# A selective-scan and mixture-of-experts kernel on one core: the part ahead of the first scan in another order, and the LayerNorm passes of batch 0 dealt out over more slots

## What is computed

```
h = in_proj_w @ ctx            # per batch: 1024 channels x 1024 time steps, contraction 512
u = silu(conv1d_4taps(h) + conv_b)
dt_lo, B, C = split(x_proj_w @ u)           # 32, 16 and 16 rows
delta = softplus(dt_proj_w @ dt_lo + dt_proj_b);  A = -exp(A_log)
state[t] = exp(delta*A)*state[t-1] + delta*u*B[t]      # 16 states for each channel
y = (sum_n C[n]*state[n] + D*u) * silu(z),   z = layernorm(x)        # "LN1"
x = x + y^T
x = x + expert_ffn(layernorm(x))            # "LN2": logits, top 2 of 8, GELU, w3
```

## Time and profile before

| | |
|---|---|
| three runs | 2397.72, 2400.32, 2401.14 us (median 2400.32) |
| profiled execution | 2398.25 us, its span 2395.8 us |
| busy: PE, DVE, ACT, POOL | 2085.5, 2036.6, 1609.8, 1542.7 us |
| mean granted TensorE clock | 0.939 |
| chain that ended last | PE 46%, DVE 18%, issue 16%, ACT 15%, POOL 4% |

### The profile page before, as it was taken

The page is one execution under the profiler, slowest core; times in us unless marked ns, Lnnn a source line. Parts: engine busy times, 40 slices in busy tenths (PEclk is TensorE's granted clock), DMA queues, the critical chain, the costliest instruction groups (busy, mean ns, idle before and its releaser), DMA issues.

```text
span 2395.8 us, 34926 instructions
## 1 busy us (share of the span) xinstructions
PE 2085.5 (87%) x11828; PEld 1308.9 (55%) x11828; DVE 2036.6 (85%) x2540; ACT 1609.8 (67%) x2381; POOL 1542.7 (64%) x1089
## 2 busy tenths in 40 slices
PE   7798889988978987998978997798887897797999
PEld 2677677766654553445665554344665454344444
DVE  5899799989997899999998899998999789899311
ACT  2687877767769869656759967855677757854500
POOL 0598777778765765667766675676776577577111
PEclk9899989998989988998989998999898998899999
DMA  5311625664612844566722653566552265478512
GB/s 179 125 45 53 222 79 159 194 211 165 233 53 102 304 149 129 176 208 220 260 66 90 238 186 124 168 220 208 198 198 67 69 227 167 151 226 290 203 62 70
DMA packets 201891, 388.93 MB, mean 162 GB/s; under 512 B 30801, under 2 KB 96337, under 8 KB 201714
## 3 DMA queue, kind: packets, MB, share of 16 engines
q1 hardware_dynamic: 198544, 386.23, 48.0%
q10 hardware_dynamic: 3170, 0.47, 0.1%
HBM read 352.56 MB, written 34.08 MB: 161 GB/s over the span
## 4 chain that ended last, share of the span: by engine, by line
PE 46%; DVE 18%; issue 16%; ACT 15%; POOL 4%; DVEq 0%; DMA 0%; ACTq 0%; POOLq 0%; SPq 0%
PE dense L1243 12%; PE dense L1060 9%; DVE h L1624 8%; PE dense L1046 5%; PE dense L1000 5%; ACT dA L1350 4%; DVE dense L1600 3%; PE dense L1226 3%; POOL h L942 3%; ACT L1319 2%; PE dense L1021 2%; DVE u L1463 2%; PE dense L1012 2%; PE dense L1163 2%; PE dense L1067 2%
## 5 line engine op out<-in xcount | busy, mean ns | idle before, releaser
L942 POOL TENSOR_TENSOR h<-h,Cb 128x1024 f32<-128x1024 f32 x512 | 1209.2, 2362 | 359.3 <-DVE h L1624 333.3
L1350 ACT ACTIVATE dA<-delta,Av 128x512 f32<-128x512 f32 x1024 | 700.1, 716 | 336.0 <-DVE h L1624 333.2
L1624 DVE TENSOR_TENSOR_SCAN h<-dA,state,dense 128x512 f32<-128x512 f32 x512 | 627.9, 1265 | 20.5 <-PE dense L1060 9.6
L1624 DVE TENSOR_TENSOR_SCAN h<-dA,dense 128x512 f32<-128x512 f32 x512 | 596.9, 1205 | 40.0 <-PE dense L1060 22.8
L1060 PE MATMUL dense<-ident,h 128*128 128x128 f32 x4096 | 570.2, 289 | 42.4 <-POOL h L942 42.2
L1060 PEld LDWEIGHTS dense<-ident,h 128*128 128x128 f32 x4096 | 496.4, 150 | 177.5 <-issue 89.5
L1600 DVE TENSOR_TENSOR dense<-dense,Bb 128x512 f32<-128x512 f32 x720 | 458.7, 683 | 0.8
L1046 PE MATMUL dense<-Bb,duT 128*128 128x128 f32 x2432 | 354.6, 296 | 108.9 <-DVE h L1624 104.1
L1046 PEld LDWEIGHTS dense<-Bb,duT 128*128 128x128 f32 x2432 | 317.4, 205 | 161.2 <-issue 159.6
L1243 PE MATMUL dense<-w3h,xT 128*128 128x512 f32 x832 | 384.8, 598 | 0.8 <-DVE xT L1581 0.8
L1243 PEld LDWEIGHTS dense<-w3h,xT 128*128 128x128 f32 x832 | 148.9, 193 | 138.7 <-issue 137.4
(11 more groups left out here) (169 smaller groups left out, 2046.1 us busy)
## 6 DMA issues: line engine op xcount, KB each, us to landing
sww<-in_sw SPq DMA_DIRECT2D x167, 512.0 KB, 4.2
Cb<-bc_scratch SPq DMA_DIRECT2D x64, 512.0 KB, 6.9
Bb<-bc_scratch SPq DMA_DIRECT2D x59, 512.0 KB, 5.0
w3h<-in_sw SPq DMA_DIRECT2D x52, 512.0 KB, 8.4
w3h<-in_w3T SPq DMA_DIRECT2D x52, 512.0 KB, 5.0
row<-x_scratch SPq DMA_DIRECT2D x40, 512.0 KB, 4.7
xz<-in_x SPq DMA_DIRECT2D x64, 256.0 KB, 4.6
xt<-in_x SPq DMA_DIRECT2D x64, 256.0 KB, 4.2
```

What stands on the lines that cost most here:

```text
L942: e.tensor_tensor(h[:, s:s + 2, :], h[:, s:s + 2, :], Cb[:, 2 * q:2 * q + 2, :], ALU.mult).then_inc(prod_done, 1)
L1350: e.activation(dA[:, i % RA, :], delta[:, st % 2, :], ACT.Exp, scale=Av[:, j * N + n:j * N + n + 1]).then_inc(dA_done, 1)
L1624: e.tensor_tensor_scan(h[:, 2 * ((PAIRS * g + q) % RH) + n % 2, :], dA[:, (N * g + n) % RA, :], dense[:, BANKS.bank[("product", g, n)], :] ...
```

## The change

It has three groups of edits.

1. **Order ahead of the first scan.** TensorE begins with 13 matmuls on the constant tile `ones`, into bank M1, which nothing reads. Then all eight in_proj blocks, then all eight x_proj pieces, the first softplus matmul, the transposes of B, and only then in_proj of J and J+1 (bank F2 instead of F1), the turn of du, now in bank S. The transposes of B go to bank YT, so they wait for the convolution of block 4, and the first sum in YT waits for VectorE's diagonals. ScalarE does the first tap of the next block ahead of a silu; table load and exp(A_log) come before the row split; the first taps of J and J+1 move into slots 0 and 1 of step 0. VectorE keeps three LN1 rows between the convolutions, does rows 3 to 6 behind the last, and row 7 behind the softplus; the convolutions of J and J+1 move between the scans of slots 1 and 2.
2. **Diagonals.** VectorE makes only four (`DVE_DIAGONALS`), those of pairs 1 and 2. For pairs 4, 5 and 6 B is loaded and GpSimd makes them, as in later halves, in slots 0 to 3 behind the product with C. There are 14 loads in place of 11.
3. **LN1 of batch 1, made during batch 0.** The passes stand in slots 57, 58, 66, 69, 71, 74, 77 and 79, power in 83 and shift in 85. The first row load of batch 0's logits moves from slot 80 to 82. Batches 1 and 2 keep their slots.

```diff
+DVE_DIAGONALS = 2 * 2
+FIRST_LN1_ROWS = ((54, 57), (55, 58), (60, 66), (63, 69), (67, 71), (70, 74), (72, 77), (75, 79))
+WARM = 13
...
-        uses = [FIRST_S + 1, 2, 2, 1, 1, 1, 1, 1]
+        uses = [FIRST_S + 1, 2, 1, 2, 1, 1, 1, 1]
...
-                rows.append((b, 54 + 3 * k // 2, "ln1", k))
-                self.add(b, 57 + 3 * k // 2, "ln1_stats", k)
-            self.add(b, 69, "ln1_rstd")
-            self.add(b, 71, "ln1_shift")
+                load, t = (54 + 3 * k // 2, 57 + 3 * k // 2) if b else FIRST_LN1_ROWS[k]
+                rows.append((b, load, "ln1", k))
+                self.add(b, t, "ln1_stats", k)
+            self.add(b, 69 if b else 83, "ln1_rstd")
+            self.add(b, 71 if b else 85, "ln1_shift")
...
+        def by_dve(c, n):
+
+            return c == 0 and on_pe(0, n) and diag_index(0, n) < DVE_DIAGONALS
...
# GpSimd
+                if c == 0:
+                    e.wait_ge(diag_done, 1 + DVE_DIAGONALS)
...
             edges(0)
+            du_of(0, 1 + FIRST_S + 1)
             ln1_rstd(0)
-            du_of(0, 1 + FIRST_S + 1)
...
-                        if j == 0 and at == SLOTS + q and c and on_pe(g, n):
+                        if j == 0 and at == SLOTS + q and on_pe(g, n) and not by_dve(c, n):
                             diagonal_b(c, n)
...
# TensorE
+            e.wait_ge(masks, 1 + MASKS)
+            for i in range(WARM):
+                e.matmul(dense[:, M1, 0:P], ones[:], ones[:], start=True, stop=True)
             e.wait_ge(ctx_loaded, 1 + 16)
             for G in range(J):
                 e.wait_ge(first_win_loaded[G], 1 + 16)
                 first_in_proj(G, G, first_win[G], ctxs)
-                if G >= 2:
-                    first_x_proj(G - 2)
-            first_x_proj(J - 2)
...
+            for k in range(J):
+                first_x_proj(k)
             e.wait_ge(ident_step, 3)
             before_softplus(0, 0, FIRST_S)
...
             turn_b(0, FIRST_S)
+            e.wait_ge(first_ctx_loaded, 1 + 16)
+            for G, bank in ((J, F0), (J + 1, F2)):
+                e.wait_ge(win_loaded[G % 2], 1 + 16)
+                e.wait_ge(evac[bank], 1 + 1)
+                first_in_proj(G, bank, win[:, G % 2], first_ctx)
+            e.wait_ge(evac[S], 1 + FIRST_S + 1)
+            turn_du(0, S)
             times_b_at(2)
...
# ScalarE
-            for G in range(J):
-                tap_one(G, G, 0, 0, G)
-                silu_u(G, G, 1)
-            tap_one(J, F0, 0, 1, 0)
-            split_rows(0)
+            for G in range(J + 1):
+                if G < J:
+                    tap_one(G, G, 0, 0, G)
+                if G:
+                    silu_u(G - 1, G - 1, 1)
...
+                    if g == 0 and q == 0:
+                        copy_du(0)
+                        copy_duT(0, S)
+                    if g == 0 and q in (0, 1):
+                        tap_one(J + q, (F0, F2)[q], 0, 1, q)
...
# VectorE
             for G in range(J):
                 first_conv(G, G)
-                first_ln1_stats(G)
-            first_conv(J, F0)
+                if G < 3:
+                    first_ln1_stats(G)
+            for k in range(3, J - 1):
+                first_ln1_stats(k)
...
             softplus_c(0, 0, FIRST_S)
-            first_conv(J + 1, F1)
+            first_ln1_stats(J - 1)
...
             for n in range(N):
-                if on_pe(0, n):
+                if by_dve(0, n):
                     diagonal_b(0, n)
```

More of the change, by code:

```diff
@@ L642, in load_bc @@
             def load_bc(c, q):
-                for i, dst in ((N, Cb),) if c == 0 and on_pe(0, 2 * q) else ((0, Bb), (N, Cb)):
+                for i, dst in ((N, Cb),) if by_dve(c, 2 * q) else ((0, Bb), (N, Cb)):
                     e.dma_start(dst[:, 2 * q:2 * q + 2, :], bc_d[c:c + 1, i + 2 * q:i + 2 * q + 2, :]
@@ L1382, in slot @@
                             silu_u(J, F0, 2)
[L1383 removed]
+                            silu_u(J + 1, F2, 2)
                         elif G < ALL:
```

39 lines of the change are left out of this document (15 added, 24 removed).

## The result

| | kernel before | changed kernel |
|---|---|---|
| time, median | 2399.45 us (4 runs) | **2384.85 us** (2376.84 to 2387.82, 4 runs) |
| ratio, 95% interval | 1 | **0.9938** [0.9923, 0.9953] |
| profiled execution: time, span | 2398.25, 2395.8 us | 2376.84, 2375.1 us |
| mean granted clock in it | 0.939 | 0.948 |

Faster by 14.6 us, forecast 15 (2385.0 us, range 2377 to 2394).

What follows compares the result with a forecast made beforehand. TensorE bounds the start, then a serial stretch of small things, and ScalarE the end of step 7. Terms -10.7 - 7.7 + 4.3 - 1.0 = -15.1 us gave 2385 us on the median's level, range 2377 to 2394.

Steps and rivals of the forecast that it cites:

- Warm-up and in_proj: Start of kernel: warm-up gains 1.05 us; last x_proj ends at 53.4 us instead of 59.68, gain 6.3 us.
- First softplus: From x_proj's end to the first softplus's end: 5.1 us instead of 5.9, ending at 58.5; gain so far 7.05 us.
- To scan 6: From first softplus to scan 6, which starts at 77.3 us instead of 87.99; gain 10.7 us including everything before it.
- Six diagonals to GpSimd: First block, four slots: 3.8 us of GpSimd work taken to cost 0; loads 3 us later would lose a microsecond each.
- LN1: End of step 7: stretch of 34.69 us falls to 27, gain 7.7; the five passes moved to later slots give 4.3 back.
- The shift: LN1's shift moved from slot 71 to 85: cost 3.6 us instead of 4.6, gain 1.0 us.
- Rival (b): Two late in_proj blocks at half clock: wholly so costs 6.9 us on the path to duT, 2392 us; chance 0.12.

Runs made afterwards that it cites:

- no_warm: Changed kernel without the 13 warm-up matmuls on the constant tile: -12.24 us against the kernel before, ratio 0.9941.
- silu_first: Changed kernel with each block's silu ahead of the next block's first tap on ScalarE again: -9.23 us against the kernel before, ratio 0.9959.
- dve_ten: Changed kernel with all ten diagonals of the first block on VectorE again: -6.55 us against the kernel before, ratio 0.9968.
- twice_after: Changed kernel with an added in-place copy ahead of each of the eight LN1 passes of the first batch: -7.63 us against the kernel before, ratio 0.9967.
- shift_87: Changed kernel with LN1's power in slot 85 and shift in 87 instead of 83 and 85: -6.98 us against the kernel before, ratio 0.9965.
- deal_early: Changed kernel with LN1 passes in slots 57, 58, 61, 64, 67, 71, 74, 78 and shift in 87: -12.32 us against the kernel before, ratio 0.9941.
- prefix_only: Changed kernel with batch 1's LN1 passes, power and shift back in their old slots: -8.56 us against the kernel before, ratio 0.9956.
- xproj_between: Changed kernel with x_proj dealt out between the in_proj blocks again, two blocks behind: -8.98 us against the kernel before, ratio 0.9960.
- the repeat: Changed kernel run once more, unchanged, for its spread: -12.71 us against the kernel before, ratio 0.9941.

## Why the prediction was right, point by point

1. **Warm-up and in_proj: right.** x_proj ends at 53.16, and the row copy behind it starts at 53.24 (53.4). Inside it the warm-up was mis-sized: 2.4 us by no_warm's profile where I had 1.05, because without it the 64 instructions took 30.78 us, 3.0 more than at the full pace of 3.47 a block, where the earlier trace rows had given 2.1. The number of slow instructions at the start differs: seven in no_warm came about 0.85 us or more apart, four in the kernel before, and the rest 0.43. (That they ran at half clock is inferred from this pace; the recorded granted clock is 1.00 there in both.) And the step rested, unpriced, on ScalarE's order: I wrote that the last silu is there at 50.2 (measured 50.04) without asking what in the change made that so. silu_first shows it: without the tap ahead of the silu it is there at 53.8. Convolutions 0 to 5, which I had done by 43, were done at 42.5.
2. **First softplus: right.** Its end is 57.64 + 0.69 = 58.33 (58.5), lead 7.22 (7.05).
3. **To scan 6: mechanism right, 1.4 us too small.** It starts at 75.86 (77.3). TensorE's late blocks end at 63.06 (63.2). The six taps, four scans and two products from 66.28 to 75.86 take 9.6 us; I had summed their durations, 10.9 with a wait for dA. Neighbours on VectorE overlap by about 0.1 each (the tap at 66.28 lasts 0.75, the scan begins at 66.94), and no wait came. Lead 12.1, not 10.7.
4. **Six diagonals to GpSimd: right**, cost 0, shown by dve_ten from the other side (3.8 us on VectorE). I said there would be no wait for the B rows. GpSimd got to its first diagonal at 68.93, earlier than the 70.9 that I had for the second product, and waited 1.63 us for a load until 70.56 (I had it landing at 69.3); nothing behind it was late.
5. **LN1: right.** 27.45 in the first stretch (27). Given back: 28.16 against 30.77 less the 4.6 of the shift, 2.0; and 29.91 - 27.65 = 2.3. Together 4.3, as written. twice_after shows the mechanism: added work is free in slot 66, and in a pair two slots apart it is paid for. In the changed kernel each pair costs a wait of 1.28 us for dA and one of 0.67 for a first tap, 1.95 where I took 2. Slot 74, for which I took 0.3, has no wait behind it; the 0.3 us more in the third stretch is in VectorE's busy time (27.69 against 27.38).
6. **The shift: direction right, size wrong.** It cost 1.45 + 0.17 = 1.6 and not 3.6, so the gain was 3.0. I had taken the 2.30 us to return because power and shift kept their distance; what decides is which instruction GpSimd takes up just before the shift, and behind the power of slot 83 that was a 128x1 one. (The aside that the sum would be 1.3 lower without the 2.30 us is a slip: 1.3 is the cost that would have been left, and the sum would have been 2.3 lower.) The rule of the Trainium skill, "SBUF — State Buffer", "Who interferes with whom", was given as a matter of which starts first. Three cases agree with it: 2.30 us before, 2.32 in shift_87 and 0.65 in deal_early, each ending with GpSimd's product. The changed kernel's 0.17 us does not show the exclusion. The 128x1 product had started first there too, and by its row it outlasted the shift by 0.3 us, so this length is what was measured and not what the rule gives.

Rival (b) did not come in the changed kernel's two profiles (1.00 in 53.5 to 63.5) but did in five of nine profiles of kernels with its prefix or a variant of it (0.83 in prefix_only, no_warm, xproj_between and deal_early, 0.67 in silu_first), with part of the 6.9 us only: the 16 instructions took 8.63 us in no_warm, 9.59 in silu_first, 7.13 in the changed kernel. prefix_only and deal_early have the very instructions of the changed kernel up to here. So this rival is a matter of the single execution, and that it stayed away from the changed kernel's two profiles is luck, not foresight.

**Where the sum agreed by luck.** In the profiles the structure gives 12.1 + 6.1 = 18.2 us, 3 more than my sum (1.4 in step 3, 2.0 in step 6, -0.3 in the rest). The medians give 14.6 and 12.7. Two errors of the sum, in steps 3 and 6, were made up for by something that I had not priced. In the repeat's profile the granted clock behind step 12 is part of it. The same stretch of work in the kernel before and in the changed kernel's repeat:

```profile
1710.07:1741.28 31.21, 28.25 (x261) 19.77 (x260) 30.36 (x43) 22.16 (x35) 22.81 (x21) 1.00 0.70 254
```

```profile
1696.10:1728.79 32.69, 29.32 (x258) 21.10 (x260) 30.45 (x42) 22.17 (x35) 24.17 (x22) 0.95 0.67 242
```

VectorE and ScalarE do the same, the clock is 0.95 instead of 1.00, and 1.5 us are gone. From step 12 to the last softplus the repeat lost 3.3 us of its lead, and the first profile won 4.4 (19.8 to 24.1). I had written 1 or 2 us for it.

All fourteen profiles do the same work from step 12's softplus maximum to the end. It took 1997.7 us in the kernel before, 1996.8 and 2002.2 in the changed kernel, and 1996.7 to 2005.2 in the others: a spread of 8.5 us, in which two profiles of one kernel lie 5.4 apart. The thirteen average 2000.0, 2.3 us longer than the one profile of the kernel before, and most of that (2.2) lies behind the last softplus. Whether the new prefix costs something there or the kernel before had a good execution, fourteen profiles don't tell. So it is shown that the later part varies by execution, by more than I allowed; it is not shown why the medians are 3.6 and 5.5 us short of the 18.2.

## What to carry to other kernels

Price an operation that is moved by where it lands: the same 1.08 us of ScalarE cost nothing in slots 66 and 74 and about 1.09 us each in 69, 71, 77 and 79, depending on how much lead its consumer has left there, and not on the engine's idle time in the stretch. When blocks pass through several engines, add up the ring (A waits for B, B for A's previous block). Compare its period with the bound engine's, and ask too whether it is short enough to work off a backlog; idle time on each engine of the ring does not mean that its order is free. A tiny instruction of VectorE that takes microseconds is to be read against what GpSimd has running: move it to where GpSimd does small things, and read the result in its duration as well as in its wait.
